# A graph network of four layers: indirect transfers of 127 rows instead of 128 in the last 84 of 196 columns

## The reference

```python
# layer 0
m = relu(x[src] + edge_attr_48);  y = (1 + eps) * x + segment_sum(m, dst)
# layer 1: degrees of src and dst, then
agg = segment_sum(x[src] * ci[src], dst) * cj;  h = where(in_deg > 0, agg, x);  y = relu(h @ W.T + b)
# layer 2: sums by the SOURCE node
agg = segment_sum(norm * x[dst], src);  y = relu(agg @ W.T + b)
# layer 3: a gate from an MLP on edge_attr_40, embeddings and distances; sums by src again
agg = segment_sum(gate * x[dst] * (cw * mj), src) / segment_sum(mj, src);  y = layernorm(x + agg) * gamma + beta
```

## Time and profile before

| | us |
|---|---|
| median of two runs | 3289.29 |
| lowest and highest run | 3288.33, 3290.25 |
| span of the profiled execution, first to last instruction | 3576.0 |
| POOL busy in the span | 2221.4 |
| VectorE (DVE) busy in the span | 2026.8 |
| TensorE (PE) busy in the span | 781.8 |
| ScalarE (ACT) busy in the span | 638.4 |

### The profile page before, as it was taken

One profiled execution on the slowest core, in us unless ns is written; L12 is line 12 of the kernel. 1 busy time (PEld: TensorE's weight loads), 2 busy tenths in 40 slices (PEclk: granted clock), 3 DMA queues, 4 the chain that ended last, 5 costly groups with the idle time before them and its releaser, 6 DMA issues. The chain is left out here.

```text
span 3576.0 us, 20072 instructions
## 1 busy us (share of the span) xinstructions
PE 781.8 (22%) x3476; PEld 557.2 (16%) x3476; DVE 2026.8 (57%) x2511; ACT 638.4 (18%) x949; POOL 2221.4 (62%) x2104
## 2 busy tenths in 40 slices
PE   1180000003666457675220000000022200000000
PEld 0020000003565434443220000000021200000000
DVE  2196798776665634455347377776542336667551
ACT  0000022112232323332110011123311101111110
POOL 5605657722655755541777777767747777774776
PEclk7595555555555555555555555555555555555555
DMA  3108656621332311119108455533300012320000
GB/s 101 19 8 281 211 176 244 213 83 37 119 105 101 110 22 23 22 22 56 24 13 58 101 209 207 206 119 96 94 28 15 15 47 62 93 63 8 14 14 15
DMA packets 167631, 308.78 MB, mean 86 GB/s; under 512 B 89258, under 2 KB 119370, under 8 KB 167474
## 3 DMA queue, kind: packets, MB, share of 16 engines
q1 hardware_dynamic: 104882, 256.60, 23.4%
q0 software_dynamic: 62720, 51.89, 7.4%
HBM read 144.86 MB, written 165.71 MB: 87 GB/s over the span
## 5 line engine op out<-in xcount | busy, mean ns | idle before, releaser
L454 POOL DMA_INDIRECT ring<-x_table,idx x392 | 448.2, 1143 | 139.7 <-issue 122.5
L465 POOL DMA_INDIRECT x_table<-sumb,idx x392 | 444.0, 1133 | 141.1 <-issue 114.2
L1205 DVE TENSOR_REDUCE var<-sq 128x28 f32<-128x1344 f32 x147 | 223.4, 1551 | 271.6 <-ACT sq L581 268.1
L776 PE MATMUL psG<-ident,tail 128*49 128x128 f32 x9 | 4.0, 446 | 1237.9 <-DVEq L959 1237.9
L465 POOL DMA_INDIRECT out<-sumb,idx x196 | 227.1, 1159 | 69.8 <-issue 58.3
L454 POOL DMA_INDIRECT ring<-xa_table,idx x196 | 221.8, 1132 | 70.5 <-issue 59.4
L454 POOL DMA_INDIRECT ring<-edge_records,idx x196 | 219.8, 1122 | 69.8 <-issue 60.9
L465 POOL DMA_INDIRECT y_table<-sumb,idx x196 | 210.7, 1075 | 68.4 <-issue 61.8
L443 POOL COPY idx<-put 128x14 int32 (+1 forms) x56 | 26.2, 469 | 355.1 <-ACT sumb L608 355.1
L454 POOL DMA_INDIRECT ring<-y_table,idx x196 | 201.7, 1029 | 68.3 <-issue 57.7
L581 ACT ACTIVATE sq<-du 128x1344 f32<-128x1344 f32 x126 | 163.9, 1319 | 415.1 <-DVE du L1199 392.0
(11 more groups left out here) (259 smaller groups left out, 3040.0 us busy)
## 6 DMA issues: line engine op xcount, KB each, us to landing
x_table<-do SPq DMA_DIRECT2D x84, 672.0 KB
din<-in_xaux SPq DMA_DIRECT2D x56, 728.0 KB
din<-x_table SPq DMA_DIRECT2D x56, 672.0 KB
xa_table<-din SPq DMA_DIRECT2D x28, 728.0 KB
y_table<-GX SPq DMA_DIRECT2D x28, 672.0 KB
x_copy<-do SPq DMA_DIRECT2D x28, 672.0 KB
din<-x_copy SPq DMA_DIRECT2D x28, 672.0 KB
out<-do SPq DMA_DIRECT2D x28, 672.0 KB
```

The costliest lines, as they stand in the source:

```text
L454: pool.indirect_dma_start(ring[:, h, t, 0:w], None, table, bass.IndirectOffsetOnAxis(ap=idx[:, h, t:t + 1], axis=0)).then_inc(fill[h].sem, ...
L465: pool.indirect_dma_start(table, bass.IndirectOffsetOnAxis(ap=idx[:, h, t:t + 1], axis=0), stage[:, h, t, :], None, bounds_check=last_row, ...
L1205: V.tensor_reduce(var[:, h, :], sq[:, h, :, :], X, ALU.add).then_inc(S["var_ready"], 1)
```

## The change

Every pass is cut into two loops. The first runs over `FULL = 4` trips (112 columns) with all 128 partitions, the second over the other 3 trips (84 columns) with the first 127 partitions of the indices and of the buffer. All ten passes do it, so 840 of the 1,960 transfers carry 127 rows. In a scatter the two turns ahead of the loop stay as they are. For layers 2 and 3 partition 127 must hold padding in the order by source too; so the key now moves the lower half of the nodes (`is_lt`, `65536 + HALF_NODES`, offset `256 - HALF_NODES`) and the upper half, padding last, ends the order. Decoding the key changes its constants alike. The sort and the decoding have as many instructions on tiles of the same shapes as before. The rest of the diff is blank lines. In the cut below, `turn` is the body of the gather's loop.

```diff
+FULL = (E - (P - 1) * CE + R - 1) // R
-            def gather(table, w, of):
+            def gather(table, w, of, less=P):
...
+                def turn(i, h, rows):
+                    pool.wait_ge(ring_free.sem, ring_free.up())
+                    indices(h, 2 * i + h, of)
+                    for t in range(H):
+                        pool.indirect_dma_start(
+                            ring[0:rows, h, t, 0:w], None, table,
+                            bass.IndirectOffsetOnAxis(ap=idx[0:rows, h, t:t + 1], axis=0)
+                                ).then_inc(fill[h].sem, fill[h].add())
+
+                with loop(pool, FULL, {own: 2, ring_free: 2, fill[0]: H, fill[1]: H}) as i:
                     for h in range(2):
...
+                        turn(i, h, P)
+                with loop(pool, NBLK - FULL, {own: 2, ring_free: 2, fill[0]: H, fill[1]: H}) as i:
+                    for h in range(2):
+                        turn(i + FULL, h, less)
...
-                        table, bass.IndirectOffsetOnAxis(ap=idx[:, h, t:t + 1], axis=0),
-                        stage[:, h, t, :], None, bounds_check=last_row, oob_is_err=False
+                        table, bass.IndirectOffsetOnAxis(ap=idx[0:rows, h, t:t + 1], axis=0),
+                        stage[0:rows, h, t, :], None, bounds_check=last_row, oob_is_err=False
...
+                scatter_turn(table, 0, 0, True, P)
+                scatter_turn(table, 1, 1, False, P)
+                with loop(pool, FULL - 1, {own: 2, rows_ready: 2, sc[0]: H, sc[1]: H}) as i:
+                    scatter_turn(table, 2 * i + 2, 0, False, P)
+                    scatter_turn(table, 2 * i + 3, 1, False, P)
+                with loop(pool, NBLK - FULL, {own: 2, rows_ready: 2, sc[0]: H, sc[1]: H}) as i:
+                    scatter_turn(table, 2 * (i + FULL), 0, False, less)
+                    scatter_turn(table, 2 * (i + FULL) + 1, 1, False, less)
...
-                one(V.tensor_scalar(vb[0:SORT_P, :], va[0:SORT_P, :], float(HALF_NODES), float(65536 - HALF_NODES),
-                                    ALU.is_ge, ALU.mult))
+                one(V.tensor_scalar(vb[0:SORT_P, :], va[0:SORT_P, :], float(HALF_NODES), float(65536 + HALF_NODES),
+                                    ALU.is_lt, ALU.mult))
```

More of the change, by code:

```diff
@@ L445, in indices, with scatter_turn @@
                 pool.sem_inc(S["pool_turns"], 1)
-            def gather(table, w, of):
-                with loop(pool, NBLK, {own: 2, ring_free: 2, fill[0]: H, fill[1]: H}) as i:
-                    for h in range(2):
[L451 to L457, removed]
+            def gather(table, w, of, less=P):
[8 more added lines that the diff above has]
+                with loop(pool, FULL, {own: 2, ring_free: 2, fill[0]: H, fill[1]: H}) as i:
+                    for h in range(2):
+                        turn(i, h, P)
+                with loop(pool, NBLK - FULL, {own: 2, ring_free: 2, fill[0]: H, fill[1]: H}) as i:
+                    for h in range(2):
+                        turn(i + FULL, h, less)
                 for h in range(2):
                     pool.wait_ge(fill[h].sem, fill[h].now())
-            def scatter_turn(table, c, h, first):
+            def scatter_turn(table, c, h, first, rows):
                 pool.wait_ge(rows_ready.sem, rows_ready.up())
@@ L471, in scatter_turn, with scatter @@
                         pool.sem_inc(S["stage_free"], 1)
[L473 to L479, removed]
+            def scatter(table, less=P):
+                scatter_turn(table, 0, 0, True, P)
[6 more added lines that the diff above has]
+                    scatter_turn(table, 2 * (i + FULL) + 1, 1, False, less)
                 pool.wait_ge(sc[1].sem, sc[1].now())
@@ L504, in _ @@
             pool.wait_ge(edges.sem, edges.up(6))
-            gather(A["xaux"], XW, srcI)
+            gather(A["xaux"], XW, srcI, P - 1)
             pool.wait_ge(S["xa_done"], 1)
-            gather(XA, XW, dstI)
+            gather(XA, XW, dstI, P - 1)
             pool.wait_ge(idx_ready.sem, idx_ready.up())
             pool.wait_ge(short_done.sem, short_done.up())
-            scatter(Y1)
-            gather(Y1, D, srcI)
+            scatter(Y1, P - 1)
+            gather(Y1, D, srcI, P - 1)
             pool.wait_ge(short_done.sem, short_done.up())
-            scatter(X2)
+            scatter(X2, P - 1)
             pool.wait_ge(idx_ready.sem, idx_ready.up())
-            gather(X2, D, srcI)
+            gather(X2, D, srcI, P - 1)
             pool.wait_ge(rec_st.sem, rec_st.up(1 + NBLK))
             pool.wait_ge(idx_ready.sem, idx_ready.up())
-            gather(REC, RW, dstI)
+            gather(REC, RW, dstI, P - 1)
             pool.wait_ge(short_done.sem, short_done.up())
             pool.wait_ge(idx_ready.sem, idx_ready.up())
-            scatter(X3)
-            gather(X3, D, dstS)
+            scatter(X3, P - 1)
+            gather(X3, D, dstS, P - 1)
             pool.wait_ge(short_done.sem, short_done.up())
-            scatter(OUT)
+            scatter(OUT, P - 1)
         @block.scalar
@@ L995, in sort @@
                 one(V.memset(vb[96:P, :], 3.4028234e38))
-                one(V.tensor_scalar(vb[0:SORT_P, :], va[0:SORT_P, :], float(HALF_NODES), float(65536 - HALF_NODES),
-                                    ALU.is_ge, ALU.mult))
-                one(V.scalar_tensor_tensor(va[0:SORT_P, :], va[0:SORT_P, :], 256.0, vb[0:SORT_P, :], ALU.add, ALU.add))
+                one(V.tensor_scalar(vb[0:SORT_P, :], va[0:SORT_P, :], float(HALF_NODES), float(65536 + HALF_NODES),
+                                    ALU.is_lt, ALU.mult))
+                one(V.scalar_tensor_tensor(va[0:SORT_P, :], va[0:SORT_P, :], float(256 - HALF_NODES), vb[0:SORT_P, :], ALU.add, ALU.add))
                 vi = vb[0:SORT_P, :].bitcast(I32)
@@ L1364, in _ @@
             one(V.tensor_copy(zs[:, :], zs[:, :].bitcast(I32)))
-            one(V.tensor_scalar(keyn[:, :], zs[:, :], 65536.0, -float(65536 - HALF_NODES), ALU.is_ge, ALU.mult))
-            one(V.scalar_tensor_tensor(key[:, :], zs[:, :], -256.0, keyn[:, :], ALU.add, ALU.add))
+            one(V.tensor_scalar(keyn[:, :], zs[:, :], 65536.0, -float(65536 + HALF_NODES), ALU.is_ge, ALU.mult))
+            one(V.scalar_tensor_tensor(key[:, :], zs[:, :], float(HALF_NODES - 256), keyn[:, :], ALU.add, ALU.add))
             one(V.tensor_copy(srcI[:, :], key[:, :]))
```

## The result

| | kernel before | changed |
|---|---|---|
| median, us | 3289.29 | 4939.03 |
| lowest to highest | 3288.33 to 3290.25 | 4938.95 to 4939.12 |
| span of the profiled execution | 3576.0 | 4937.2 |

The ratio is 1.502, with a 95% interval of 1.4976 to 1.5064. The predicted 3293 us, and the range up to 3450, missed it by far.

The account below looks back on a forecast made before the run. It took POOL's pace to bound seven of ten passes. In the profiled execution 3576.0 - 5.2 + 5 + 4 = 3579.8 us; the change times 0.92, added to the median 3289.3, gave 3293 us, range 3110 to 3450.

Parts of the forecast that it names:

- What bounds the kernel: Whole kernel: POOL, busiest at 2221.4 us, sets the pace in seven of ten passes, 588 of 840 changed transfers.
- I count these three as covered: Gather of in_xaux, scatter to Y1, gather from Y1: POOL waits for ScalarE (121.4, 67.4, 91.3 us), so changes there cost nothing.
- a factor of 0.92: Whole kernel: scale applied to changes in the profiled execution, span 3576.0, to forecast changes of the median 3289.3 us.
- Part 1: 588 late transfers on the path: one row fewer saves 8.9 ns each, 5.2 us in all.
- Part 2: Second loop of each pass: new program text may arrive late, at most +15 us, taken as +5 us.
- Part 3, POOL side: POOL's writing of a 127-row list: between -447 and +700 us over 588 transfers, taken as the same duration as 128.
- Part 3, DMA side: Wait for each pass's last transfer: +2.0 us if one engine carries all rows, +14 at most, taken as +4 us.
- Rival A: Late columns of seven passes: one DMA engine carries each transfer and falls behind, +357 us, 3646 us; chance 0.20.
- Rival B: POOL's list writing: a list for one engine is cheaper, -135 us (3155) or -206 us (3084); chance 0.28.
- rival C: Changed transfers: 127 treated as 16 shares of 8, the last of 7, 3289 us; half of the likeliest case's 0.52.
- B's first sum: Cheaper one-engine lists on POOL, saving 0.25 us for each of 588 transfers: -135 us, given as 3155 us.

## Why the prediction was wrong, step by step

- **What bounds the kernel: right, but too weak.** POOL was named, and it is. The step "I count these three as covered" failed. The span of the profiled execution, 3576.0, exceeded the median by 287 us, and I carried that over as a factor of 0.92 on everything. It was not a factor: it was extra waiting in the first half. The kernel with split loops and 128 rows needs 149 us for the first 112 transfers of the first pass, the trace of before 252, while from 1676 on the early and the late stretch of every pass agree within 2 us. The 105.7 us wait in the earlier trace rows is no part of the 3289 us. The changed kernel's trace has no such wait, nor have the four of the chip where the kernel before takes 3288 us; the six traces of the chip where it takes 3607 all have it, with 106 to 113 us. So the trace that I read was one of the longer kind. Where the kernel takes 3289 us, nearly all of the added work of all ten passes is on the path.
- **Part 1, 5.2 us for one row fewer: wrong.** No row has a price by itself; an entry in each of 16 lists costs 13 ns.
- **Part 2, +5 us for the second loops: wrong, 0.** The long waits for issue are not program text that arrives late. The split kernel with 128 rows has them as the kernel before does, in eight of its ten passes after 113 transfers, where its second loop starts after 112. Before a first transfer of 127 rows the stop comes after 112, and then after every 7. Where they come changes with the number of rows alone, so they go with what has been put into the lists.
- **Part 3, POOL side: the step that decided, and it failed.** I set the price of making the list between -0.76 and +1.2 us and took the transfer of 128 itself, "the same duration". It is +1.59 us, 2.533 against 0.940, outside my bounds: the longest gather of the trace, 2329 ns, was one of 128 rows like all others and no bound for another kind of list. In the sum this is +1259 us of POOL's time where I had 0. Add the stops, 4.2 us in the mean for seven transfers, for which I had no term: +469 us.
- **Part 3, DMA side: half right.** The waits for the last transfer of a scatter grew from 1.6 and 1.7 us to 4.1 at most, near the 2.0 us that I had added for each, and did not matter. The number of packets changes, but it rises to 112 in a quiet scatter instead of falling to 17, since all 16 engines get entries.
- **Rival A had the right sign and cause, the divisor, at the wrong place.** It let one DMA engine fall behind. Its sign, transfers of 2 us or more without VectorE, did come, but the engines are idle between transfers; it is POOL that is slow. Its highest price, +357 us, was under a quarter of the loss. The rule set beside it, of the Trainium skill's page "DMA: Bandwidth & Descriptors", section "Why a DMA increments its semaphore by 16 and not by 1", is one engine for 127 partitions. By the bytes and the packet sizes it holds for these indirect transfers. It was named and then given only 0.20. The same skill's page "Perfetto Trace Analysis", section "DMA Instruction — SWDGE (GPSIMD)", says that such an instruction ends in the profile when its descriptors are written. The trace agrees: the smallest duration is 2534 ns for rows of 48 values and 2533 for rows of 52, and it grows with the entries.
- **Rival B, a cheaper list, is refuted,** and so is rival C, 16 shares with the last one short, by the same rows. (B's first sum, 3289 - 135, is 3154 and not 3155; nothing hangs on it.)

## What to carry to other kernels

The row count of an indirect transfer is not a size but a shape: keep it a multiple of 16, or at least a count with a large divisor up to 16, and let padding rows ride along. Dropping one row of 128 raised the price from 0.94 to 2.53 us, while 126 rows cost 0.98. When a change meets a case that no row of the trace shows, don't set the case equal to the nearest row because it looks near, and don't take the longest row for a bound. And a profiled span that stands off the timed median by 9% calls for the question in which stretch it was lost, before any of its waits is called cover.

## What the runs showed of the hardware

- POOL's time for an indirect transfer is about 0.87 us plus 13.1 ns for each entry in one list (2.533 = 0.87 + 127 x 0.0131), where the list length is the row count divided by its largest divisor up to 16. Short lists lie near it (8 entries: 0.97 by the line, 0.940 measured).
- All 16 engines get a list of that length. Those without rows get entries of 4 bytes: for 127 rows of 192 bytes 75 packets of 88 bytes and 15 of 68 in each transfer.
- POOL stands still for a few us when enough entries have been put in. With lists of 127 it does so every 7 transfers. With lists of 31 it does after 28 transfers and with lists of 61 after 14, counted from the stop before the first of them, in eight of ten passes; the other two have no such stop there. The products, 889, 868 and 854, are alike, but lists of 97 waited after 10 and then after every 14, where I had expected 9 or 7. With lists of 127, in the last three passes, POOL goes on 0.9 to 1.4 us after the queue has run empty. That some store of fixed size must be emptied is my reading; its size and what the stop is for stay open.
- The kernel before takes 3288 us on one chip and 3607 on another. Its trace of 3576 us, set beside that of the split kernel with 128 rows (3286 us), has the difference in the stages before 1700 us, and not in the speed of the indirect transfers. What makes it stays open.
